# First feed-forward of a four-batch decoder kernel: gate by ScalarE's Silu, and the second batch's delta behind its gates

## The reference, cut to what matters

```python
def bit_linear(x, w, b):
    gamma_x = jnp.clip(jnp.max(jnp.abs(x), axis=-1, keepdims=True), 1e-05, None)
    scale_x = 127.0 / gamma_x
    x_dq = jnp.clip(jnp.round(x * scale_x), -128.0, 127.0) / scale_x
    ...
    return jnp.einsum('bsd,hd->bsh', x_ste, w_ste) + b
gate = jax.nn.silu(bit_linear(x, gate_w, gate_b))
val = bit_linear(x, val_w, val_b)
return bit_linear(gate * val, out_w, out_b)
```

## Time and profile before

| what | value |
|---|---|
| median of 3 runs | 1866.79 us |
| profiled execution, its own time, given as its span | 1867.3 us |
| TensorE busy | 1758.7 us, 94% |
| VectorE busy | 1317.8 us, 71% |
| ScalarE busy | 955.9 us, 51% |
| GpSimd busy | 663.5 us, 36% |
| HBM traffic | 126 GB/s over the span |

### The profile page before, as it was taken

How to read it: one execution, slowest core, us unless ns; L and a number is a source line. 1 busy time by engine, 2 the same in 40 slices (tenths; PEclk the granted TensorE clock), 3 DMA queues, 4 the chain that set the end, 5 groups by cost and what they waited for, 6 DMA issues and landing times.

```text
span 1867.3 us, 19387 instructions
## 1 busy us (share of the span) xinstructions
PE 1758.7 (94%) x6054; PEld 801.7 (43%) x6054; DVE 1317.8 (71%) x1919; ACT 955.9 (51%) x1904; POOL 663.5 (36%) x693
## 2 busy tenths in 40 slices
PE   8878769989999999999999999999999899999999
PEld 2323233434444344444444544444444344454543
DVE  3978877998998799889887989987643444422221
ACT  6867875656563555575456565564435233330100
POOL 1324522345472244456432464562123333310100
PEclk9989889999999899999999999999999999999999
DMA  8999933688771146697312589841112799846110
GB/s 267 260 289 291 300 109 98 173 211 215 189 195 46 48 102 155 160 266 196 102 31 70 129 199 234 212 109 62 41 47 78 215 301 256 246 141 241 68 51 28
DMA packets 163173, 300.30 MB, mean 161 GB/s; under 512 B 18936, under 2 KB 51704, under 8 KB 160128
## 3 DMA queue, kind: packets, MB, share of 16 engines
q1 hardware_dynamic: 145792, 236.14, 40.3%
q0 software_dynamic: 17280, 62.92, 17.5%
HBM read 177.64 MB, written 58.33 MB: 126 GB/s over the span
## 4 chain that ended last, share of the span: by engine, by line
PE 62%; DVE 18%; issue 6%; ACT 5%; DMA 5%; POOL 2%; SPq 2%; DVEq 0%; ACTq 0%; POOLq 0%
PE p L799 9%; PE p L776 8%; PE p L759 8%; PE p L810 8%; PE p L846 6%; DVE s_M L963 5%; PE p L652 4%; PE p L782 4%; PE p L861 3%; DVE s_M L958 2%; PE p L699 2%; DVE s_M L968 2%; PE p L733 2%; DMA s_bc<-bc_scratch 1%; PE p L738 1%
## 5 line engine op out<-in xcount | busy, mean ns | idle before, releaser
L963 DVE TENSOR_TENSOR_SCAN s_M<-s_M 128x1024 f32<-128x1024 f32 x128 | 296.8, 2319 | 7.8 <-ACT s_M L1218 5.3
L1106 DVE CUSTOM_DVE_ANT_0 s_U<-p,s_U 128x512 f32<-128x512 f32 x256 | 187.3, 745 | 162.8 <-PE p L776 161.5
L776 PE MATMUL p<-s_U 128*128 128x512 f32 x512 | 269.3, 614 | 5.6 <-DVE s_U L1106 2.8
L759 PE MATMUL p<-s_U 128*128 128x512 f32 x512 | 253.7, 604 | 4.7 <-DMA s_U<-in_Wq 2.1
L1445 POOL DMA_DIRECT2D s_u<-s_M x120 | 112.6, 938 | 391.5 <-DVE s_M L968 368.8
L1490 POOL TENSOR_SCALAR s_U<-s_U 128x512 f32<-128x512 f32 x256 | 229.4, 917 | 6.3
L810 PE MATMUL p<-s_U 128*128 128x512 f32 x512 | 224.0, 593 | 0.0
L799 PE MATMUL p<-s_U 128*128 128x512 f32 x472 | 213.6, 593 | 2.6 <-ACT s_U L1348 2.5
L1348 ACT COPY s_U<-p 128x512 f32<-128x512 f32 x196 | 105.3, 592 | 189.7 <-PE p L782 188.4
L1218 ACT ACTIVATE s_M<-s_dl,s_small 128x511 f32<-128x511 f32 x256 | 170.3, 718 | 40.3 <-DVE s_M L963 36.8
L1343 ACT ACTIVATE s_U<-s_U 128x512 f32<-128x512 f32 x256 | 181.6, 710 | 5.3
(11 more groups left out here) (171 smaller groups left out, 2364.3 us busy)
## 6 DMA issues: line engine op xcount, KB each, us to landing
s_u<-s_M POOLq DMA_DIRECT2D x120, 512.0 KB, 7.6
s_bc<-bc_scratch SPq DMA_DIRECT2D x128, 256.0 KB, 5.0
k_scratch<-s_U SPq DMA_DIRECT2D x16, 1024.0 KB, 9.4
v_scratch<-s_U SPq DMA_DIRECT2D x16, 1024.0 KB, 7.8
s_U<-in_Wq SPq DMA_DIRECT2D x64, 256.0 KB, 6.9
s_U<-k_scratch SPq DMA_DIRECT2D x64, 256.0 KB, 5.2
s_U<-rk_scratch SPq DMA_DIRECT2D x64, 256.0 KB, 5.5
s_U<-in_Wo SPq DMA_DIRECT2D x64, 256.0 KB, 4.5
```

The costliest lines, as they stand in the source:

```text
L759: ins = e.matmul(banks[bk][:], wqq[j % 2][:, k, :], axT[b % 2][:, k, :], start=(k == 0), stop=(k == 3))
L776: e.matmul(banks[bk][:], qT[j % 3][:, k * 128:(k + 1) * 128], kT[j % 2], start=True, stop=True).then_inc(S["a_s"], 1)
L963: e.tensor_tensor_scan(w, dA[i % 2], w, 0.0, ALU.mult, ALU.add).then_inc(S["m_s"], 1)
L1106: e.tensor_tensor_reduce(out=Pm[j % 2][:, k, :], in0=banks[ABANK[kind, j, k]][:], in1=rkb[j % 2], scale=rq[:, k:k + 1], scalar=-3.0e38, op ...
```

## The change

Four things change, for the first batch (b = 0) unless said otherwise. The gate is computed by one Silu on ScalarE with the full scale, the VectorE pass (tanh + 1) * gate is left out, and the two row scales are formed to match; the gate bank is then free as soon as ScalarE has read it. In the planner, the second batch's softplus ("sp") needs the first feed-forward's last gate. TensorE's first gate product waits for 8 instead of 12 quantized parts, the waits for all 12 move to VectorE's first product and TensorE's first output product; the normalization and the load of the bias rows lose theirs. The planner's costs for the chunk parts on VectorE are new: 0.8 and 1.9 us for the first batch and 1.5 and 2.3 us for the others, instead of 2.3 us for each.

```diff
--- before.py
+++ after.py
@@ -231,7 +231,7 @@
         elif kind == "dt":
             part((kind, i), [("PE", 1.0), ("ACT", 0.7)], ("xp", 4 if b else 3), take=own, free=own)
         elif kind == "sp":
-            part((kind, i), [("ACT", 3.3)], ("dt", 3))
+            part((kind, i), [("ACT", 3.3)], ("dt", 3), *([(0, "m", 3, 6)] if b == 1 else []))
         elif kind == "soft":
             part((kind, i), [("DVE", 1.25)], ("sp", 0), *([(0, "put", 2, 3)] if b == 1 else []))
         elif kind == "init":
@@ -271,12 +271,12 @@
         if kind == "m":
             pair = [("g", t, k // 2), ("v", t, k // 2)]
             if k % 2:
-                part(name, [("DVE", 2.3)], ("m", t, k - 1), free=pair)
+                part(name, [("DVE", (2.3 if k % 4 == 3 else 1.5) if b else (1.9 if k % 4 == 3 else 0.8))], ("m", t, k - 1), *([] if b else [(0, "put", 2, 3)]), free=pair)
             else:
-                part(name, [("PE", 2.6), ("ACT", 0.7)], ("e", t, 2), take=pair)
+                part(name, [("PE", 2.6), ("ACT", 0.7)], ("e", t, 2), *([] if b else [(0, "put", 1, 3)]), take=pair)
         elif kind == "e":
             if k == 0:
-                part(name, [("DVE", 1.0), ("POOL", 1.1)], ("yt", 3), *([] if b else [(0, "put", 2, 3)]))
+                part(name, [("DVE", 1.0), ("POOL", 1.1)], ("yt", 3), *([] if b else [(0, "bias", 0, 2)]))
             elif k == 1:
                 part(name, [("DVE", 4.4)], ("e", t, 0))
             else:
@@ -671,14 +671,14 @@
                             e.wait_ge(S["f_x"], 4 * b + t + 1)
                             if t == 0 and b == 0:
                                 e.wait_ge(S["d_rows"], 32)
-                                e.wait_ge(S["q_put"], 12)
+                                e.wait_ge(S["q_put"], 8)
                         g, v = LBANK[b, "g", t, ch], LBANK[b, "v", t, ch]
                         vacant(g)
                         vacant(v)
                         bias(t, g, ch, 0)
                         bias(t, v, (ch + 1) % 4, 512)
                         product(t, g, ch, wqg).then_inc(S["f_g"], 1)
-                        freed[g] = (S["f_p"], i + 1)
+                        freed[g] = (S["f_p"], i - 15) if b else (S["f_th"], i + 1)
                         product(t, v, ch, wqv).then_inc(S["f_v"], 1)
                         freed[v] = (S["f_h"], i + 1)
                     elif kind == "l" and k in (1, 2):
@@ -693,6 +693,8 @@
                             freed[bk] = (S["f_hc"], 16 * b + 4 * t + k4 + 1)
                     elif kind == "l" and k == 3:
                         e.wait_ge(S["f_hc"], 16 * b + 4 * t + 4)
+                        if t == 0 and b == 0:
+                            e.wait_ge(S["q_put"], 12)
                         bk = LBANK[b, "o", t]
                         vacant(bk)
                         for i in range(16):
@@ -1014,7 +1016,7 @@
                         rowstat(xt, qt[:, 0:2], qt[:, 2:8], "f_rv")
                     elif kind == "e" and k == 1:
                         if t == 0 and b == 0:
-                            e.wait_ge(S["q_put"], 12)
+                            e.wait_ge(S["d_rows"], 16)
                         e.wait_ge(S["f_rs"], 8 * b + t + 1)
                         e.tensor_scalar(xn, xt, qt[:, 0:1], qt[:, 1:2], ALU.subtract, ALU.mult).then_inc(S["f_hn"], 1)
                         e.wait_ge(S["f_hn"], f + 1)
@@ -1041,15 +1043,23 @@
                                 e.tensor_scalar(gsc[:, k3:k3 + 1], gam[:, k3:k3 + 1], (0.5, 2.0)[k3] / 127.0, None, ALU.mult).then_inc(*v.up())
                             e.tensor_scalar(gsc[:, 2:3], gam[:, 2:3], gts[:, 2:3], 1.0 / 127.0, ALU.mult, ALU.mult).then_inc(*v.up())
                             e.wait_ge(*v.now())
-                        e.tensor_scalar(qt[:, 12:13], qt[:, 10:11], gsc[:, 0:1], None, ALU.mult).then_inc(*v.up())
-                        e.wait_ge(*v.now())
-                        e.scalar_tensor_tensor(qt[:, 13:14], qt[:, 10:11], gsc[:, 1:2], qt[:, 12:13], ALU.mult, ALU.mult).then_inc(S["f_sc"], 1)
+                        if b:
+                            e.tensor_scalar(qt[:, 12:13], qt[:, 10:11], gsc[:, 0:1], None, ALU.mult).then_inc(*v.up())
+                            e.wait_ge(*v.now())
+                            e.scalar_tensor_tensor(qt[:, 13:14], qt[:, 10:11], gsc[:, 1:2], qt[:, 12:13], ALU.mult, ALU.mult).then_inc(S["f_sc"], 1)
+                        else:
+                            e.tensor_scalar(qt[:, 12:13], qt[:, 10:11], gsc[:, 0:1], 2.0, ALU.mult, ALU.mult).then_inc(*v.up())
+                            e.tensor_scalar(qt[:, 13:14], qt[:, 10:11], gsc[:, 1:2], None, ALU.mult).then_inc(S["f_sc"], 1)
+                            e.wait_ge(*v.now())
                     elif kind == "m" and k % 2 == 1:
                         ch, i = k // 2, 4 * f + k // 2
                         ti = tt[i % 2]
                         e.wait_ge(S["f_th"], i + 1)
-                        e.scalar_tensor_tensor(ti, ti, 1.0, banks[LBANK[b, "g", t, ch]][:], ALU.add, ALU.mult).then_inc(S["f_p"], 1)
-                        e.wait_ge(S["f_p"], i + 1)
+                        if b:
+                            e.scalar_tensor_tensor(ti, ti, 1.0, banks[LBANK[b, "g", t, ch]][:], ALU.add, ALU.mult).then_inc(S["f_p"], 1)
+                            e.wait_ge(S["f_p"], i - 15)
+                        elif i == 0:
+                            e.wait_ge(S["q_put"], 12)
                         e.wait_ge(S["f_sc"], f + 1)
                         e.wait_ge(S["f_v"], i + 1)
                         if ch == 0 and f:
@@ -1267,7 +1277,7 @@
                             e.wait_ge(S["f_sc"], f + 1)
                         if i >= 2:
                             e.wait_ge(S["f_h"], i - 1)
-                        e.activation(tt[i % 2], banks[LBANK[b, "g", t, k // 2]][:], ACT.Tanh, scale=qt[:, 12:13]).then_inc(S["f_th"], 1)
+                        e.activation(tt[i % 2], banks[LBANK[b, "g", t, k // 2]][:], ACT.Tanh if b else ACT.Silu, scale=qt[:, 12:13]).then_inc(S["f_th"], 1)
                     elif kind == "l" and k in (1, 2):
                         for k4 in (2 * k - 2, 2 * k - 1):
                             if k4 == 0 and f:
```

## The result

The changed kernel takes 1902.44 us (median of 4 runs, 1899.26 to 1907.65) against 1866.72 for the one before on the same chip: ratio 1.0202, 95% interval 1.0184 to 1.0221. The forecast was 1862.3, with a range from 1850 to 1874. The change costs 36 us, and the prediction had the wrong sign.

What follows compares the result with a forecast made beforehand. TensorE was taken as the bound, with gains only in its idle time or low clock. Passes and waits counted zero, the handover −4.5 us, the late second mamba nothing within its margin: 1866.8 became 1862.3 us, range 1850 to 1874.

Steps and rivals of the forecast that it cites:

- Part 2: Moved waits for quantized weights before the first feed-forward: already met before they were reached, worth zero, ends 0 and −1 us.
- Part 1: First batch's 16 dropped gate passes, 10.8 us of VectorE: direct worth zero, since keys and values cover them on TensorE.
- Table loads: ScalarE: two loads of 1.28 us between last gate and first decay, none inside the gates; three up to that decay.
- When the gates end is the unknown. I take 340: First feed-forward's last gate: 335 at the earliest, 345 with key products slipped in now and then, 340 taken.
- The rival (c): Slower: second mamba's late start is paid at the 17th query, D about 16.6 us, time 1874.4; chance 0.20.
- First scan at about 348: Second batch's first scan on VectorE, behind gate, table loads, softplus, product and decays: about 348 instead of 335.4.
- D = 3: Lateness of the second mamba, from 45.7 us of VectorE room against 48.5 needed: 3 us, between −2 and +8.
- The margin of 9.0 us: Second batch's turned rows are ready at 731.9, the 17th query starts at 740.88: 9.0 us of lateness cost nothing.
- The handover, −4.5 us: Keys to attention: normalized-rows wait goes, 4.4 us query-weights wait comes; first query 407.4 instead of 411.88; ends −8.9 and 0.
- The waits inside the first head ... stay: Start of attention: waits inside the first head and its 1.7 us of low clock stay, as no filler is left.
- ±3 us for the costs of the later batches: New planner costs reorder later work by little, with 40.2 us of idle time there: ±3 us allowed in each case.
- The table-load rule: Skill's extra 1.38 us drain per ScalarE table switch would make D 5.8 and the move −3.2; the prediction did not adopt it.

Runs made afterwards that it cites:

- kernel 3: Changed kernel with the planner's needs and costs put back, so every engine has the old order; Silu, dropped passes and moved waits stay: 1868.09 us, ratio 1.0000.
- kernel 8: Changed kernel with the planner's chunk costs of the later batches back at 2.3 us: 1894.15 us, ratio 1.0138.
- kernel 6: Kernel 5 with the last four of 16 key and value units held in the planner until the last gate: 1897.71 us, ratio 1.0154.
- kernel 9: Kernel before the change, with the second batch's softplus needing the third tile's last gate (12th of 16): 1874.73 us, ratio 1.0046.
- kernel 1: Kernel before the change, with only the planner need of the second batch's softplus for the last gate; Tanh, passes, costs stay: 1903.43 us, ratio 1.0206.
- Kernel 5: Changed kernel, first query planned behind the last value product, first scores behind the last norm's transfer instead of the last key store: 1889.55 us, ratio 1.0132.
- kernel 7: Kernel before the change, with only the new planner chunk costs (1.5 or 2.3 us) for batches 1 to 3: 1873.40 us, ratio 1.0040.

## Why the prediction was wrong

**The waits on weights (Part 2): right.** The first gate starts at 279.7, before at 279.9.

**The passes that go (Part 1): right.** Direct worth zero, and kernel 3 measures 1.0000 in the old order. A Silu gate takes 0.69 us, as Tanh did. In the late order the rest of the change was worth 9.3 us (kernel 8), which the prediction didn't have.

**Table loads: right.** Two between the last gate and the first decay, at 364.23 and 374.31, none between gates; with the one at 239.6, ahead of the gates, they are the three of the forecast.

**"When the gates end is the unknown. I take 340": this is the step that failed.** It was 363.5. The 335 to 345 were a count of TensorE's work: 55 us of it up to the last gate (335), and with 340 5 us more for "a key product slipped in now and then". From 280 to 363.5 TensorE never idles in the changed kernel, and 32.0 of its 83.5 us are key and value products; the other 51.5 are near the 55 of the forecast. So the term that was mis-sized is the 5 us. Why so much slips in, kernel 6 shows: with those products held back the gates still ended only at 355.6, with 10.4 us of idle time from 280 on and a lower clock. The feed-forward is a chain through VectorE and ScalarE that leaves gaps, and the planner fills them. Holding the products back wins 7 to 8 us of the 23.5; the other 15 or so stay, as waits and as low clock. VectorE's waits from 280 to 401 in the changed kernel, in us, times and longest, say the same from the other side:

```profile
DVE s_U L1069 <- PE p L652: 26.5, 8, 5.4
```

VectorE waits for the products and TensorE, when it is left empty, for VectorE. The rival (c) named this ("VectorE with nothing to do during the gates") and had the sign; its 16.6 us were too few because it took the same 340. (The 16.6 aren't what its own terms give either: 12.6 from 335.4 to 348 and 6 for late rows are 18.6.)

**"First scan at about 348": 377.0.** 23.5 of the 29 are the gates' end. The rest lies between: from the last gate to the first scan it takes 13.5 us, not 7.8, as ScalarE's 6.9 us of other work stand between softplus and the decays' table load. I had counted the instructions of the chain and none of what the order puts among them.

**D = 3, "between −2 and +8": 40.6.** The scans' delay was to be recovered with VectorE's idle time, but idle time before the first scan can't be used by scans. Behind it there was little: 12.18 us of what there was went to the decays held up by the first query.

**The margin of 9.0 us: right, as a statement about rows.** In the four kernels where the turned rows of the second batch come more than 15 us late, the 17th query's lateness is theirs less 9.0, within 2.1 us: 27.5 against 27.7 measured, 31.0 against 33.1, 19.7 against 19.9, 17.8 against 18.0; and in kernel 9, 0.3 against 0.5. It says nothing where something else is late: with keys held back the rows are 1.1 us late and the query 22.3, since attention began 24 us late. What was wrong is that D, the last scan's delay, arrives in full at the rows: of 18.7 only 9.3 do, of 33.6 26.8, of 40.6 36.5, and of 20.4 in kernel 6 only 1.1. With the measured D the forecast's own formula gives 40.6 − 9.0 = +31.6 and 1898; the measurement is 1902.4. That this comes so near is in part luck: the delay shrinks on its way to the rows, and the handover and the later batches' costs, which the formula doesn't have, add. For kernel 1 it is 8 us short, for kernel 6 20. The mechanism was in the prediction, with a D wrong by a factor of more than 13.

**The handover, −4.5 us: right in its first step alone.** The wait for normalized rows went and the wait for query weights came, but at 9.14 us, not 4.4. Two things add: the issue sat 3.0 us behind a load of B and C rows, and one value product instead of two covered it (8.1 + 3.0 − 2.0 = 9.1). What I missed is what stands behind the first query on ScalarE: decays, and with them the scans and the second head. "The waits inside the first head ... stay" was false; the third query is 19.6 us late. Late scans meant that the handover was full of decays and scans, in three engines' queues at once. Kernel 5 puts the price of this part at 12.9 us (1902.44 − 1889.55, from two runs; the last scan comes 7 us earlier there, which is part of it).

**±3 us for the costs of the later batches: too small.** 7.6 us alone (kernel 7), 8.3 in the change (kernel 8). The sum of 40.2 us of idle time left after 440 bounded what could be won, and I used it as though it bounded what could be lost.

**The table-load rule: not what decided.** The load ends at 365.51 and softplus starts at 365.53. The 1.38 us of drain that the Trainium skill adds to a load ("ScalarE: Activation LUTs", "What ACT_TABLE_LOAD costs") isn't seen at either load behind the last gate: the gap ahead of a load is 17 to 18 ns and the one behind it 11 to 12. The 19 us of extra loads in kernel 3 cost nothing measurable.

Open is where the last part of the loss comes from. The changed kernel is 27.7 us late at the 17th query and 38.5 at the last; the difference is 1.4 us in kernel 1, 4.2 in kernel 5, 6.7 in kernel 9, 7.0 in kernel 7. The new costs make it larger in kernel 7, and in the changed kernel against kernel 8 (there 4.5 with the old ones), but no single wait carries it. About half of it lies in one place: from the 25th to the 32nd query's copy it takes 194.9 us before and in kernel 1, and 200.6 in the changed kernel, 200.2 in kernel 7 and 199.6 in kernel 9, with 1.7 to 3.9 us more of TensorE's idle time. No run was made for it.

## What to carry to other kernels

A need added to a planner is a delay: price it against the slack at the place where the delayed result is used, and take the delay from the whole chain of the work waited for (its hops over the engines, tile by tile), not from the busiest engine's sum, which is only a lower bound. When a late chain is pushed into a handover, read each in-order queue there for what would stand behind its waits. And time taken off an engine that has cover was worth nothing in the old order; in the late one the rest of the change gave back 9.3 us of the 37.7 that the ordering cost. An ordering made to collect such time has to be priced by itself first.

## What the runs showed of the chip

- A TensorE that was left waiting paid twice. With keys held back it idled 10.3 us of 65, and the gates' matmuls took 429 ns each against 380, at a granted clock of 0.90 against 1.00. The first query after the 9.14 us wait took 6.54 us instead of 3.67, at 0.59 against 1.00.
- 15 more table loads of 1.28 us at gates and decays (kernel 3) moved the end by nothing measurable (1.0000, 0.9978 to 1.0022), on a ScalarE that is busy for half of the span.
- A change of the planner's costs, which alters the order of instructions and none of them, moved the kernel by 7.6 us (kernel 7).
